# Four attention layers on one core: first layer recomputed in fewer products, third layer's projection folded into its values, reciprocals as logarithm and exponential, maxima turned by transfers, all of the last layer's sums on POOL

## The chip, the cores and the metric

The kernel runs on one core of a Trainium2 chip. The time is the device time of one execution in microseconds. Six engines matter: PE (TensorE, matrix products), DVE (VectorE), ACT (ScalarE), POOL (GpSimd), SP (SyncE, which here only issues transfers) and the DMA engines. Each runs its own list of instructions in order; they meet through semaphores.

## The reference

Eight images of 256 channels and 1024 positions go through four layers. Each layer adds to or replaces `x`, and each holds a softmax over 1024 by 1024 scores. Cut to what is computed:

```python
# layer 0 (L = 32 latent channels, P = 128 concepts)
th, ph, g = conv1x1(x, w_theta), conv1x1(x, w_phi), conv1x1(x, w_g)
lat = softmax(th.T @ ph) @ g.T              # (1024, 32), then reshaped as (32, 1024)
sa = gamma_sa * conv1x1(lat, w_o) + x
enc = conv1x1(sa, w_theta)
lat2 = softmax(enc.T @ concepts.T) @ concepts   # again reshaped
x = gamma_moca * conv1x1(lat2, w_o) + sa
# layer 1
q, k, v = Wq @ x + bq, Wk @ x + bk, Wv @ x + bv         # 32, 32, 256 channels
x = gamma * (v @ softmax(q.T @ k).T) + x
# layer 2
h = group_norm(x); q, k, v = qkv_w @ h + qkv_b          # 256 channels each
x = x + proj_w @ (softmax(q.T @ k / 16) @ v.T).T + proj_b
# layer 3: 8 heads of 32 channels
h = group_norm(x); q, k, v = per head of wq h + bq, wk h + bk, wv h + bv
o = softmax(q.T @ k) @ v for each head
x = layer_norm(wo @ o + bo) * ln_gamma + ln_beta + x
```

The reshape of the latents in layer 0 is not a transpose: a (1024, 32) array is read as (32, 1024), so that the elements change their place among partitions and columns.

## The kernel before

**Tiling.** An image lies in SBUF as 128 partitions by 2 channel halves by 1024 columns. PSUM is one tensor `ps` of 8 banks of 512 fp32 columns. Banks 0 to 3 belong to the layers 0 to 2 ("front"), banks 4 to 7 to layer 3 ("back"). Every attention works on tiles of 128 keys (`NT` = 8) and two halves of 512 queries (`IC` = 2). Scores are made with the keys on the partitions, exponentiated by ACT into SBUF (`pr` in front, `prb` in back) and used as the moving operand of a product with the values. The sum over the keys is gathered by elementwise additions of these tiles (`acc`, `accb`) and one product with ones at the end of each half (`sum_weights`, L690 in front, L869 in back). The numerators are divided by this sum afterwards.

**Exact scores.** Queries and keys are split into a high and a low part (to_stacks, low_stacks, high_parts, low_parts). In layers 0, 1 and 3, three such parts are stacked on 96 partitions, and row 96 (`ROW`) holds minus the maximum of each query, so that one product of 97 rows gives the shifted score (`stacked_scores`, L544). The maxima come first: `max_tile` (L530) makes a tile of scores with the queries on partitions and DVE takes the negated maximum of 1024 columns (`maximum`, L1141), 8 per head. To get them into row 96, PE multiplies each column by the identity (`shift_rows`, L537, 8 products per head) and ACT copies row 96 of the result (`shift_row`, L931).

**Layer 0.** `values0` (L580) makes the values with 16 products of 32 columns. `weigh` (L596) weighs them in four column groups, ACT copies the parts, PE turns and adds them (L604) and sums the weights by a column of ones (L609), DVE divides (`latents`, L1159, L1162), SP writes the latents to DRAM and reads them back in the other shape (L367, L370), PE multiplies by the output weights (`times_wo`, L617) and DVE adds the input (L1173). The second half repeats this with the concepts: projection (L511), scores (L640), softmax, transposition (L646), product (L651), the DRAM trip and `times_wo` again.

**Layers 1 and 2.** `chunks` runs 4 double steps per half: PE makes two banks of scores, ACT exponentiates both in one instruction of 1024 columns (L942), PE weighs (L672), POOL adds (`add_step` L431, `fold` L437). One pair of banks is in use, so the next scores wait for the exponentials. DVE takes the reciprocal of the sums (L1191, 512 columns) and multiplies (L1195). Layer 2 then projects (L511 with `o2`) and DVE adds to `xm` (L1290).

**Layer 3.** Heads are done in two groups of four (`u` = 0, 1). For each: SP copies the parts into the stacks (L390, 24 transfers), 32 maxima, four `shift_rows`, then 16 steps (`steps(u)`): four scores into three turning banks, four exponentials (L1027), weighing of the step before in four column groups (L857). DVE adds the weights of two heads (`add_weights`, L1316) and POOL those of the other two (L485): 7 additions per half on each. ACT's exponentials of step s wait for the additions of step s-2, because `prb` holds two steps. `normalise` takes the reciprocal (L1323) and multiplies (L1327). At the end come the projection, the layer norm with its square root on ACT (L1081) and reciprocal on DVE (L1360), and the output.

**Order.** Layers 0 to 2 of batch b+1 and layer 3 of batch b are written as two generators on each engine. The table `ORDER` says, per engine, how many pieces of the one and of the other follow each other; `merged` reads it. In the last batch the back runs alone, its second group's maxima merged with the first group's steps ("last").

## Time and profile before

| | us |
|---|---|
| median of 3 runs | 3452.57 (3451.96 to 3454.35) |
| the profiled execution, time | 3459.3 |
| the profiled execution, span | 3457.5 |

| engine | busy, share of span |
|---|---|
| PE | 3090.3 us, 89% |
| DVE | 2004.5 us, 58% |
| ACT | 1174.9 us, 34% |
| POOL | 1030.6 us, 30% |

The mean granted TensorE clock is 0.857 of full speed. A window row gives a stretch in us from the start, its length, and then for each engine the busy time and the number of instructions, the granted clock (1.0 is 2.4 GHz, 0.5 is 1.2 GHz), and the DMA share and rate. A group row gives source line, engine, operation, output and inputs, shapes, count, then busy time in us and mean ns of one, then the idle time of the engine before them and what ended it. One fp32 product counts as two PE instructions.

### The profile page before, as it was taken

Reading aid. Unit: us, or ns where it says so; the run is one execution under the profiler, and the core shown is the slowest. Engines: PE = TensorE matmul, PEld = TensorE weight load, DVE = VectorE, ACT = ScalarE, POOL = GpSimd, SP = SyncE. Lnnn points to the kernel's source line nnn. Section 1 sums busy time; section 2 is a strip of 40 time slices with the busy share of each in tenths; the row PEclk is TensorE's granted clock in tenths of the full one; section 3 lists DMA queues with packets and bytes.
Section 4 is the critical chain, followed back from the end, with each engine's and each line's share of the span. In section 5 each row is a group of like instructions: output and inputs, shape, how many; then the busy total and the mean of one; then the engine's idle time right before and its main releaser. Section 6 shows DMA issues by size and latency. Waiting matters only on the chain.

```text
span 3457.5 us, 27670 instructions
## 1 busy us (share of the span) xinstructions
PE 3090.3 (89%) x10884; PEld 1609.0 (47%) x10884; DVE 2004.5 (58%) x1853; ACT 1174.9 (34%) x1736; POOL 1030.6 (30%) x435
## 2 busy tenths in 40 slices
PE   5778998989989898999989899898998989898886
PEld 2344544545445453545435454454545544354432
DVE  2242657555574656647574565746567465655576
ACT  1111251522525233342424325242243423243145
POOL 2002141411605115141233215150161422423044
PEclk7689797986989879898879979798798987899688
DMA  1000101020100201002010110102010020100300
GB/s 53 3 0 25 40 4 37 1 73 7 37 0 1 73 7 37 1 22 55 4 37 1 41 36 7 33 1 73 7 37 1 7 67 6 37 1 25 71 2 13
DMA packets 44803, 84.77 MB, mean 25 GB/s; under 512 B 24160, under 2 KB 24320, under 8 KB 43392
## 3 DMA queue, kind: packets, MB, share of 16 engines
q1 hardware_dynamic: 42496, 74.61, 8.7%
q0 software_dynamic: 2176, 8.39, 0.8%
q8 instruction: 85, 1.39, 0.2%
q14 instruction: 46, 0.38, 0.0%
HBM read 13.76 MB, written 10.49 MB: 7 GB/s over the span
## 4 chain that ended last, share of the span: by engine, by line
PE 68%; DVE 17%; ACT 6%; SPq 4%; issue 2%; POOL 1%; DMA 1%; DVEq 0%; ACTq 0%; POOLq 0%
PE ps L511 14%; PE ps L672 11%; PE ps L544 9%; PE ps L530 7%; DVE nmx_b L1141 6%; PE ps L857 6%; PE ps L765 5%; SPq L390 4%; PE ps L617 3%; PE ps L519 3%; PE ps L537 3%; DVE accb L1316 2%; DVE rden L1191 2%; PE ps L596 2%; PE ps L746 2%
## 5 line engine op out<-in xcount | busy, mean ns | idle before, releaser
L1027 ACT ACTIVATE prb<-ps 128x512 f32<-128x512 f32 x1024 | 556.5, 599 | 542.3 <-PE ps L544 474.5
L1141 DVE TENSOR_REDUCE nmx_b<-ps 128x1 f32<-128x1024 f32 x512 | 605.8, 1216 | 128.7 <-PE ps L530 127.4
L485 POOL TENSOR_TENSOR accb<-accb,prb 128x1024 f32<-128x1024 f32 x192 | 514.1, 2678 | 169.7 <-ACT prb L1027 161.5
L530 PE MATMUL ps<-ks,qs 96*128 96x512 f32 x960 | 457.1, 593 | 84.5 <-DVE nmx_b L1141 70.5
L1316 DVE TENSOR_TENSOR accb<-accb,prb 128x1024 f32<-128x1024 f32 x192 | 360.3, 1877 | 227.3 <-ACT prb L1027 225.0
L672 PE MATMUL ps<-pr,x_in 128*128 128x512 f32 x1024 | 488.5, 612 | 0.0
L485 POOL TENSOR_TENSOR accb<-prb 128x1024 f32<-128x1024 f32 x32 | 98.2, 3068 | 1164.8 <-ACT prb L1027 1111.6
L544 PE MATMUL ps<-qs,ks 97*128 97x512 f32 x960 | 393.9, 480 | 23.9 <-ACT prb L1027 12.1
L530 PEld LDWEIGHTS ps<-ks,qs 96*128 96x128 f32 x960 | 212.2, 259 | 332.3 <-DVE nmx_b L1141 254.9
L544 PEld LDWEIGHTS ps<-qs,ks 97*128 97x128 f32 x960 | 172.5, 195 | 278.6 <-ACT prb L1027 162.2
L942 ACT ACTIVATE pr<-ps 128x1024 f32<-128x1024 f32 x192 | 196.4, 1023 | 302.8 <-PE ps L544 215.5
L672 PEld LDWEIGHTS ps<-pr,x_in 128*128 128x128 f32 x1024 | 201.0, 197 | 194.4 <-issue 173.0
L857 PE MATMUL ps<-prb,vb 128*32 128x512 f32 x2048 | 278.4, 616 | 0.9 <-ACT prb L1027 0.9
L431 POOL TENSOR_TENSOR acc<-acc,pr 128x1024 f32<-128x1024 f32 x80 | 195.6, 2445 | 264.8 <-ACT pr L942 262.6
L511 PE MATMUL ps<-h,w 128*128 128x512 f32 x384 | 206.5, 690 | 40.6 <-DVE h L1195 38.2
L1141 DVE TENSOR_REDUCE nmx_f<-ps 128x1 f32<-128x1024 f32 x192 | 226.6, 1214 | 18.2 <-PE ps L746 13.7
L511 PE MATMUL ps<-hb,w 128*128 128x512 f32 x384 | 196.9, 661 | 24.5 <-ACT hb L951 22.9
L765 PE MATMUL ps<-q2k 128*128 128x512 f32 x768 | 199.7, 396 | 0.0
L431 POOL TENSOR_TENSOR acc<-pr 128x1024 f32<-128x1024 f32 x40 | 94.8, 2370 | 300.3 <-ACT pr L942 300.3
L1191 DVE RECIPROCAL rden<-ps 128x512 f32<-128x512 f32 x32 | 107.4, 3355 | 132.6 <-PE ps L690 131.2
L1323 DVE RECIPROCAL rdenb<-ps 128x512 f32<-128x512 f32 x32 | 107.3, 3354 | 100.5 <-PE ps L869 100.4
L765 PEld LDWEIGHTS ps<-q2k 128*128 128x128 f32 x768 | 146.3, 190 | 37.9 <-issue 6.0
(148 smaller groups left out, 3296.2 us busy)
## 6 DMA issues: line engine op xcount, KB each, us to landing
qs<-part SPq DMA_DIRECT2D x180, 128.0 KB, 2.3
ks<-part SPq DMA_DIRECT2D x180, 128.0 KB, 2.4
x_in<-in_x POOLq DMA_DIRECT2D x8, 1024.0 KB, 5.8
xd<-xm SPq DMA_DIRECT2D x8, 1024.0 KB, 4.6
out<-prb SPq DMA_DIRECT2D x32, 256.0 KB, 2.0
q2k<-part SPq DMA_DIRECT2D x24, 128.0 KB, 2.4
w<-in_weights SPq DMA_DIRECT2D x1, 2592.0 KB, 10.4
latents<-rden SPq DMA_DIRECT2D x16, 128.0 KB, 2.3
```

Of the source, the lines that this page charges most:

```text
L431: pool.tensor_tensor(into[:], pr[:, (s - 1) % 2, :, :] if jg == 1 else into[:], pr[:, s % 2, :, :], ALU.add).then_inc(summed[n].sem, 1)
L485: pool.tensor_tensor(accb[:, 2:4, :], prb[:, (s - 1) % 2, 2:4, :] if j == 1 else accb[:, 2:4, :], prb[:, s % 2, 2:4, :], ALU.add)\
L511: mm = pe.matmul(ps[0:m, bank, :], wcol(name, kt, m0, m), src[:, kt, cols(ic)], start=kt == 0, stop=kt == CH - 1)
L530: mm = pe.matmul(ps[:, bank + jc, :], queries[0:STACK, tile(it)], keys[0:STACK, cols(jc)], start=True, stop=True)
L544: return pe.matmul(ps[:, bank, :], keys[0:ROW + 1, tile(jt)], queries[0:ROW + 1, cols(ic)], start=True, stop=True)
L672: mm = pe.matmul(ps[:, 2 + ch, :], v[:, jt, tile(ch)], pr[:, s % 2, j, :], start=jt == 0, stop=jt == NT - 1)
L765: mm = pe.matmul(ps[:, j, :], kpart[:, kt, keys], qpart[:, kt, cols(ic)], start=False, stop=kt == CH - 1 and kpart is kl2)
L857: mm = pe.matmul(ps[L * g:L * g + L, back0 + 2, :], vb[:, jt, L * (QUAD * u + g):L * (QUAD * u + g + 1)], prb[:, s % 2, g, :], start=jt == ...
L942: act.activation(pr[:, s % 2, :, :], ps[:, 0:2, :], ACT.Exp).then_inc(exped[n].sem, 1)
L1027: act.activation(prb[:, s % 2, g, :], ps[:, turn3[score_use(s, g) % 3], :], ACT.Exp)\
L1141: dve.tensor_reduce(nmx[side][:, head, it:it + 1], ps[:, bank:bank + 2, :], AX.XY, ALU.max, negate=True).then_inc(max_sb[n].sem, 1)
L1316: dve.tensor_tensor(accb[:, 0:2, :], prb[:, (s - 1) % 2, 0:2, :] if j == 1 else accb[:, 0:2, :], prb[:, s % 2, 0:2, :], ALU.add)\
```

## The change

**Layer 0** is rebuilt. The projection gives theta twice, g and phi in one product of 128 rows; DVE copies g to SBUF and PE turns it with 8 transposes into `vgo`, whose other 32 columns are ones, so that the weighing product also makes the sums and the additions on POOL go. The parts are added by two products with two stacked identities. DVE's 32 by 32 transpose, reading PSUM in the order of the reshape, takes the place of the trip through DRAM; the reciprocal is of 32 by 32 elements. `enc` is not made from `sa`: theta of the input is kept in rows 32 to 63 of `lat_r`, and a prepared product of the output weights, theta and the concepts adds the latents' share, so the first product with the output weights, the first residual and the projection of `sa` go. One product with the output weights (`wo_con` of 64 rows, both gammas in it) does both residuals.

**Layers 1 to 3.** The value biases move behind the softmax (into `bo2`, `bo3`, and the residual of layer 1), gamma of layer 1 into its value weights, and the third layer's projection into its value weights at the start of the program; after `chunks` DVE adds straight to `xm`. `chunks` now runs single tiles, with two banks of scores taking turns and four of weights, weighing two tiles behind. ACT copies the numerators to `tmp`. Every reciprocal of sums becomes ln on PSUM and exp(-x) on ACT (`invert`); group and layer norm use ln and exp(-x/2); a table set that holds ln and exp is loaded at the start. Half of the value copies move from DVE to ACT.

**Maxima of layer 3.** DVE transposes the 128 by 32 block of maxima in blocks of 32 by 32 and rounds it; SP copies it by four transfers into row 96 of the four heads. The 64 products and 8 ACT copies per batch go.

**Sums of layer 3.** POOL does both additions of a step; DVE none.

**The next image** is loaded as soon as layer 0 has added its residual, into `x_in`, since the values of layers 1 and 2 now lie in `h`. The `ORDER` table is new for all engines.

The core of the diff:

```diff
-                pool.tensor_tensor(accb[:, 2:4, :], prb[:, (s - 1) % 2, 2:4, :] if j == 1 else
-                                   accb[:, 2:4, :], prb[:, s % 2, 2:4, :], ALU.add)\
-                    .then_inc(summed_pool.sem, 1)
+                for pair in (slice(0, 2), slice(2, 4)):
+                    pool.tensor_tensor(accb[:, pair, :], prb[:, (s - 1) % 2, pair, :] if j == 1 else
+                                       accb[:, pair, :], prb[:, s % 2, pair, :], ALU.add)\
+                        .then_inc(summed_pool.sem, 1)
```

```diff
+            def invert(b, n, count, bank, into):
+                act.wait_ge(total[n].sem, total[n].at(b, count))
...
+                act.activation(into, ps[:, bank, :], ACT.Ln).then_inc(logged[n].sem, 1)
+                yield
+                act.wait_ge(logged[n].sem, logged[n].at(b, count))
+                act.activation(into, into, ACT.Exp, scale=-1.0).then_inc(inverse[n].sem, 1)
```

```diff
+            def shift_rows(b, u, last):
+                queries = stacks3(u, last)[0]
+                sp.wait_ge(max_r[3].sem, max_r[3].at(b, u + 1))
+                for q in range(QUAD):
+                    row = queries[ROW:ROW + 1, :, :].rearrange("p g (i q c) -> p q (g i) c", q=QUAD, c=L)
+                    sp.dma_start(bf32(row[:, q, :, :]), bf32(nmx_r["back"][L * q:L * q + L, :])).then_inc(shift_in.sem, 16)
+                yield
```

```diff
-                pe.wait_ge(normed[2].sem, normed[2].at(b, 4))
-                for k in range(4):
-                    ic, ch = divmod(k, CH)
-                    project(k, "o2", h, P * ch, P, ic).then_inc(l2_proj.sem, 1)
-                yield
```

```diff
             def latents(b, n):
-                sums = ps[:, 2, 0:NT * (L + 1)].rearrange("p (n c) -> p n c", n=NT)
-                dve.reciprocal(rlat[:], sums[:, :, L]).then_inc(l0_rlat.sem, 1)
-                yield
...
+                dve.wait_ge(l0_lat_ps.sem, l0_lat_ps.at(b, n + 1))
+                dve.transpose(turned[n], ps[0:2 * L, 2 * n:2 * n + 2, :].rearrange("p i n -> p (i n)")
+                              .rearrange("p (l r) -> p r l", l=L)).then_inc(l0_turned.sem, 1)
+                yield
+                dve.wait_ge(l0_turned.sem, l0_turned.at(b, n + 1))
+                dve.reciprocal(inv_sums[n], turned[n][sums[n], :].rearrange("p (r c) -> p r c", r=L)[:, :, 0])\
+                    .then_inc(l0_inv.sem, 1)
+                yield
+                dve.wait_ge(l0_inv.sem, l0_inv.at(b, n + 1))
+                dve.tensor_tensor(lat_r[mixed[n], :].rearrange("p (r c) -> p r c", r=L),
+                                  turned[n][mixed[n], :].rearrange("p (r c) -> p r c", r=L),
+                                  inv_sums[n].unsqueeze(2).broadcast_to([L, L, L]), ALU.mult)\
+                    .then_inc(l0_lat.sem, 1)
```

```diff
+                for t in range(STEPS):
+                    ic, jt = divmod(t, NT)
+                    if t == 0:
+                        pe.wait_ge(shift_sb[n].sem, shift_sb[n].at(b, 1))
+                    scores(take_turn(use01(t)), jt, ic).then_inc(scored[n].sem, 1)
+                    yield
+                    if t > 1:
+                        weigh(t - 2)
+                        yield
```

## Rows read from the trace of the kernel before

**Rows 1.** The page: busy time, share of the span and instructions of each engine.

```profile
PE 3090.3 (89%) x10884; PEld 1609.0 (47%) x10884; DVE 2004.5 (58%) x1853; ACT 1174.9 (34%) x1736; POOL 1030.6 (30%) x435
```

**Rows 2.** Windows: one steady stretch, cut into the last layer's five stages.

```profile
1264.00:1356.00 92.00, 86.23 (x326) 39.54 (x326) 50.80 (x36) 45.41 (x77) 51.17 (x19) 0.90 0.12 28
1356.00:1426.00 70.00, 61.05 (x163) 30.95 (x162) 56.67 (x63) 11.46 (x14) 5.98 (x3) 0.76 0.04 10
1426.00:1516.00 90.00, 89.12 (x401) 50.74 (x399) 45.20 (x33) 46.29 (x76) 43.98 (x18) 1.00 0.00 1
1516.00:1561.00 45.00, 39.83 (x111) 18.62 (x110) 25.22 (x18) 14.21 (x19) 10.31 (x6) 0.92 0.14 47
1561.00:1673.50 112.50, 103.19 (x371) 58.13 (x371) 70.42 (x82) 31.16 (x35) 16.78 (x8) 0.81 0.17 43
```

**Rows 3.** Groups by form: DVE, ACT and POOL instructions that set prices.

```profile
L1141 DVE TENSOR_REDUCE nmx_b<-ps 128x1 f32<-128x1024 f32 x512 | 605.8, 1216 | 128.7 <-PE ps L530 127.4
...
L1027 ACT ACTIVATE prb<-ps 128x512 f32<-128x512 f32 x1024 | 556.5, 599 | 542.3 <-PE ps L544 474.5 <-DVE accb L1316 36.0 <-POOL accb L485 27.8
...
L485 POOL TENSOR_TENSOR accb<-accb,prb 128x1024 f32<-128x1024 f32 x192 | 514.1, 2678 | 169.7 <-ACT prb L1027 161.5
...
L1191 DVE RECIPROCAL rden<-ps 128x512 f32<-128x512 f32 x32 | 107.4, 3355 | 132.6 <-PE ps L690 131.2
...
L948 ACT ACT_TABLE_LOAD x16 | 20.5, 1283 | 0.3
```

**Rows 4.** Groups by form: PE instructions that the change removes in whole or part.

```profile
L511 PE MATMUL ps<-h,w 128*128 128x512 f32 x384 | 206.5, 690 | 40.6 <-DVE h L1195 38.2 <-ACT h L951 2.4
...
L617 PE MATMUL ps<-pr,wo_con 32*128 32x512 f32 x128 | 114.2, 1070 | 10.5 <-DMA pr<-latents 10.5
...
L537 PE MATMUL ps<-ident_r,nmx_rb 128*128 128x128 f32 x512 | 79.8, 316 | 4.5 <-DVE part L1136 1.7 <-DVE nmx_rb L1147 1.5 <-ACT qs L931 1.3
...
L511 PE MATMUL ps<-xm,w 128*32 128x512 f32 x64 | 38.8, 763 | 0.8 <-DVE xm L1173 0.8
...
L580 PE MATMUL ps<-w,x_in 128*128 128x32 f32 x256 | 29.8, 276 | 0.0
```

**Rows 5.** Timeline, PE: start and duration in us; last row with the wait before it.

```profile
1265.79 7.19 PE L617 MATMUL ps<-pr,wo_con 32*128 32x512 f32 x8
...
1284.47 1.06 PE L857 MATMUL ps<-prb,vb 128*32 128x512 f32 x8
...
1502.18 1.53 PE L765 MATMUL ps<-q2k 128*128 128x512 f32 x6
...
1512.57 3.60 PE L672 MATMUL ps<-pr,x_in 128*128 128x512 f32 x8
...
1551.82 9.33 PE L511 MATMUL ps<-h,w 128*128 128x512 f32 x16 [4.77 <-DVE h L1195]
```

**Rows 6.** One line: SP's issues of the stacks, ns min/median/max, and their landing.

```profile
L390 SPq DMA_DIRECT2D ks<-part x180: 507/591/1701, 354.2 to 3218.3; - x180
...
DMA to landing us min/median/max: 2.2/2.3/3.7
```

**Rows 7.** One line each: POOL's and DVE's additions, duration ns min/median/max.

```profile
L485 POOL TENSOR_TENSOR accb<-accb,prb x192: 2349/2398/3350, 465.8 to 3423.9; 128x1024 f32<-128x1024 f32 x192
...
L1316 DVE TENSOR_TENSOR accb<-accb,prb x192: 1207/1696/3236, 463.5 to 3421.6; 128x1024 f32<-128x1024 f32 x192
```

**Rows 8.** Windows of the head: first, second and third layer of batch 0.

```profile
23.00:127.00 104.00, 74.71 (x212) 35.98 (x213) 22.17 (x26) 17.67 (x17) 16.62 (x8) 0.63 0.03 5
127.00:207.00 80.00, 58.88 (x145) 29.92 (x144) 28.97 (x28) 13.82 (x13) 16.61 (x8) 0.80 0.00 0
207.00:342.00 135.00, 112.51 (x351) 66.86 (x352) 40.22 (x58) 23.35 (x26) 17.34 (x9) 0.90 0.04 16
```

**Rows 9.** Windows of the last batch: first round with maxima, second round.

```profile
3278.00:3362.00 84.00, 68.43 (x275) 28.57 (x275) 67.19 (x51) 36.75 (x68) 38.16 (x14) 0.84 0.08 18
...
3370.00:3431.00 61.00, 48.80 (x212) 16.01 (x212) 41.21 (x17) 34.60 (x66) 40.33 (x14) 0.87 0.00 1
```

778 lines of the change are left out of this document (403 added, 375 removed), and 22 rows, old and new, of the table ORDER.

## The prediction

> **What bounds the kernel now.** I read the page first, then the stages of one steady stretch, then the groups of instructions by form. The page [rows 1] shows PE busy 89% of the span, DVE 58%, ACT 34%, POOL 30%. So most of the time is PE's own work.
>
> The run has a head (batch 0's first three layers alone, 0 to 342 us), seven stretches in which the first three layers of batch b+1 are merged with the last layer of batch b, and the last layer of batch 7 alone (3188 us to the end). One stretch lasts 409.5 us, and [rows 2] cut one into five stages by the last layer: round one of its steps (92 us), the second group's maxima (70), round two (90), its end (45), and group norm to the first group's maxima, which is also where the first layer runs (112.5). The reader should see two kinds of stage. Round two has PE busy 89.1 of 90 us at full clock: it is PE's work and nothing else. The maxima stages have PE at a granted clock of 0.76 to 0.81 in the mean of its two levels (2.4 GHz is 1.0, 1.2 GHz is 0.5) and DVE busy 57 of 70 and 70 of 112.5. There the order is set by DVE's reductions (32 of 1.216 us are 39 us, [rows 3]), by short serial steps, and by PE at the low clock.
>
> **What goes on PE.** Per batch, each group's busy time of [rows 4] divided by 8:
> - The third layer's projection is folded into the value weights. Its 16 instructions are a third of the 48 per batch in the group of 206.5 us: 8.6 us.
> - The first layer loses its values product (29.8 / 8 = 3.7), one of two products with the output weights (114.2 / 2 / 8 = 7.1), the 32-row projection (38.8 / 8 = 4.9), and the turning of the parts and the sums by a column of ones, 32 instructions as short as the 32 of the values product: 3.7 again.
> - The last layer loses the 64 small products that spread the maxima (79.8 / 8 = 10.0).
> Removed: 8.6 + 3.7 + 7.1 + 4.9 + 3.7 + 10.0 = 38.0 us. Added: eight small transposes and two fp32 products of 512 columns for the parts, with two more in place of the sixteen 33-column ones. An fp32 product of this width is two instructions, and eight of them take 3.60 us at full clock [rows 5], so 0.45 each, 0.9 at the low clock. Four such products replace or add 3.6 to 7.2 us, minus the sixteen short ones (1.9), plus 0.9 for the transposes: 2.6 to 6.2. I take 4.5. Net 33.5 us of PE busy per batch, 268 us over eight. This is the core of the forecast. It is 8% of the span, and only in idle PE time would it be worth nothing.
>
> **What goes around PE.** The 512-column reciprocals on DVE (3.36 us each, ten per batch) become a logarithm and an exponential on ACT, each priced at the 0.599 us of the nearest ACT row: 1.2 us and one hand-over of about 0.2. Where PE waits for them this gives back some 2 us: it waited 4.77 us before the projection of the third layer [rows 5], every batch, and that wait goes with the projection. Next late there is the fourth layer's group norm, because PE goes on with the next first layer, which waits only for the last normalisation. The table loads of 1.283 us (16 in the group of [rows 3], 47 in all) disappear if one set holds all functions used. They are 60 us of ACT over the run, mostly beside other work, and I count 1 us per batch within the stages below. The Trainium skill, ScalarE: Activation LUTs, section "What ACT_TABLE_LOAD costs", puts a switch at about 2.66 us with its drain; by that the same 47 would be 125 us of ACT, and the sum would not change, since ACT is a third busy.
>
> The trip of the latents through DRAM goes: two transfers in a row, twice per batch. In the head PE idles for it; in the stretches the maxima fill it. In its place stand two DVE transposes of 64 x 1024 and two 32-partition products over 1024 columns. The trace has no such transpose. Bounds: the nearest 1024-column DVE rows give 1.22 us as the floor [rows 3], a reciprocal's pace of 6.6 ns per column gives 6.7 us as the ceiling. I take 1.3, since it writes one element per lane and column as the reduction reads one. The shift's eight ACT copies per batch go with it, and instead SP issues four transfers per group. An issue holds SP 0.59 us and lands 2.3 us later [rows 6], so 4 x 0.6 + 2.3 + 0.5 of DVE = 5.2 us from the last maximum to the first step. PE has 6.9 us (first group) and 8.6 us (second) of projections placed ahead of the steps in its order, so this is hidden in the stretches. Without that cover it would cost 5.2 where the shift products now cost 8. Queued behind it on SP are only the next stacks, which need the round's scores anyway.
>
> **What POOL pays.** The last layer's sums now split between DVE and POOL, 14 additions each per round. Afterwards POOL makes all 28. An addition takes POOL 2.349 us at least, 2.398 in the median and 3.35 at most [rows 7]; DVE's own twin runs from 1.207 to 3.236. Both are slow where they overlap, which is the trace's sign that the two engines hold each other up. With DVE's additions gone I take 2.4: 28 x 2.4 = 67 us per round. Into each round also fall three such sums of the front layer and a fold of half the width, 3.5 x 2.4 = 8.4 us. POOL starts after the second step (6 us in) and stands still for some 3 us between the two halves, until PE has summed the first one. Together 6 + 67 + 8.4 + 3 + 1 = 86 us. The Trainium skill, SBUF — State Buffer, section "Who interferes with whom", says that a DVE instruction with two SBUF inputs and a GpSimd instruction reading SBUF exclude each other for the whole instruction. The trace agrees (1.207 against 3.236 us), and by that rule POOL's 2.4 is right only while few such DVE operations are left; the new products with the inverse sums and the residual additions are eight of that kind for each of two layers.
>
> **Stage by stage, one stretch.** PE's instructions of each stage, counted from the order tables of both kernels and priced at full clock by [rows 5] (1.53 us for six one-pass products, 1.4 where more follow at once; 3.60 for four of fp32; 1.06 for a step's four weighings), come to 78 us of PE in round one before and after, 87 to 96 in round two (the new order puts more of the third layer there), 44 to 34 in the second maxima, 35 to 26.5 at the end, and 75 to 60 in the first-layer stage.
> - Round one: PE 78, POOL 86. It is now POOL's stage. 92 becomes 87.
> - Second maxima: DVE needs 39 for maxima and 10 for the front layer, and 8.6 of projections follow. 70 becomes 60.
> - Round two: PE 96, POOL 86, with steps of 3 to 4 us of PE in the first half where POOL needs 4.8, so some stall: 90 becomes 100.
> - End and first-layer stage, 157.5 together: the chain from the last sum to the fourth layer's input falls from 15 us (reciprocal, projection) to 6.5. The end keeps 30. The rest is 35 us to the first maximum and 46 of DVE (39 and the first layer's 7) plus 9 to the steps, about 91. Sum 127.5, minus 30.
> A stretch: 409.5 - 5 - 10 + 10 - 30 = 374.5, so 35 us less. Seven: 245.
>
> **Head.** [rows 8]: first layer 104 us at clock 0.63, where PE is busy only 75. Two double transfers (5.2 us of PE idle each), half of the serial chain after the weighing and the ping-pong of scores and exponentials go: 104 becomes 69. Second layer 80 becomes 65, since scores now run one bank ahead and a 3.36 us reciprocal goes. Third 135 becomes 115: projection 7, waits 8, ping-pong 5. The folded products at the start add 5. Together 65 less.
>
> **Last batch alone.** [rows 9]: the second round takes 61 us now, no front layer beside it. POOL alone is 6 + 67 + 3 = 76, so +18 with its sum. The first round, 84 us with the maxima in it, becomes about 81; the shift stages give 5, the last normalisation and layer norm (three reciprocals in a row) 8. Sum +2.
>
> **Sum.** The profiled execution's span is 3457.5 us and its time 3459.3, 0.2% over the median of 3452.57. 3457.5 - 65 - 245 + 2 = 3149.5, plus 1.8 around it 3151, and by the same 0.2% a median of 3145.
>
> **Rivals.**
> 1. POOL stays slow. DVE's remaining two-input operations and waits keep an addition at its present mean, 2.68 us [rows 3]. Then a round is 28 x 2.68 + 8.4 + 10 = 93 for POOL, round two near 104, so +10 per stretch and +8 at the end: 3225. For it: the 3.35 us maxima of [rows 7]. Against it: the overlap partner is gone. The Trainium skill, GPSIMD Engine Reference, section "4.1 Engine selection", advises VectorE for element-wise sums and calls GpSimd about 2 times slower; by the trace it is 2.35 against 1.21. At a contended 3.3 us throughout, rounds would be 110 each and the gain would go: about 3440.
> 2. The first-layer stage does not shrink. PE has less to do there, and the clock was at the low level where PE idled for DVE. If that stage is held by DVE and hops and keeps 17 of the 30 us, the time is 3145 + 119 = 3265.
> 3. Logarithm and exponential do not share a table. Twelve logarithms per batch would bring 24 loads, 31 us of ACT, half on the path: 3145 + 120 = 3265.
> 4. Slower: POOL's pace drops PE's clock. PE runs in order, so a late POOL holds the front layers too, and in both rounds PE would idle enough to be granted the low level. Their 174 us of full-clock work take 249 us at a mean clock of 0.70 instead of 187: +62 x 7, so 3580. It eats the gain of 35 per stretch from a mean clock of about 0.78 down. Against it: round one now is granted 0.90 and round two 1.00 [rows 2], and PE's share there stays near 90%.
> 5. Better: the orders fit, and the second maxima and the first-layer stage reach DVE's floor, 12 us less per stretch: 3060.
>
> **How the numbers follow.** Forecast 60%, rival 1 14% (of which 2% for the lost gain), rival 2 10%, rival 3 3%, rival 4 4%, rival 5 9%. The unknown sizes (transpose 1.2 to 6.7, POOL 2.35 to 2.68, stages by some 5 us each) give 3085 to 3225 around the forecast. To leave out no more than 2 in 10 I reach to rivals 2 and 3 and stop short of 5: 3080 to 3265. Faster by over 0.2%, about what a measurement of this kernel can tell: 95%, within 1%, slower 4%.
>
> **What would show it.** PE busy falls by 230 to 300 us; a stretch lasts 362 to 385 us; POOL busy rises to about 1210 us (8 x (56 x 2.4 + 17)) with additions near 2.4 us; POOL is among the releasers of the last layer's exponentials in round one; round one stays near 87 and round two grows; there is one table load; the last round alone grows by 15 to 20 us. The prediction is wrong if additions stay above 2.6 us, if the granted clock of the rounds drops below 0.85, or if the first-layer stage stays above 100 us.

## The result and the profile after

The changed kernel takes 3152.7 us (median of four runs, 3147.6 to 3157.4) against 3453.5 of the kernel before beside it: a ratio of 0.913, 95% interval 0.911 to 0.914. The forecast was 3145. Its profiled execution has a span of 3151.9 us; the sum of the prediction made 3149.5 of it.

The page of the changed kernel, busy time by engine, answers to [rows 1]. PE lost 297.5 us, DVE 601, and POOL gained 306:

```profile
PE 2792.8 (89%) x9636; PEld 1421.5 (45%) x9636; DVE 1403.5 (45%) x1525; ACT 1208.5 (38%) x2073; POOL 1336.3 (42%) x595
```

The same steady stretch as in [rows 2], cut at the same events (round one, second maxima, round two, end, first-layer stage), by windows. Columns: window, length, busy us and instructions of PE, PE's weight loads, DVE, ACT, POOL, then granted clock, DMA share, GB/s:

```profile
1119.90:1206.00 86.10, 79.67 (x335) 36.35 (x334) 21.57 (x20) 50.14 (x89) 75.86 (x34) 1.00 0.18 46
1206.00:1267.00 61.00, 52.11 (x122) 25.20 (x120) 52.47 (x62) 9.95 (x17) 7.25 (x4) 0.78 0.03 6
1267.00:1361.00 94.00, 94.00 (x419) 52.91 (x421) 16.27 (x16) 49.43 (x90) 75.15 (x33) 1.00 0.00 1
1361.00:1400.00 39.00, 33.52 (x89) 15.91 (x81) 18.66 (x25) 16.00 (x27) 8.14 (x4) 0.91 0.15 55
1400.00:1494.70 94.70, 81.01 (x244) 44.70 (x245) 65.42 (x69) 24.98 (x37) 0.00 (x0) 0.80 0.15 34
```

Round two has no idle PE time at all: it is PE's. Round one has POOL busy 75.9 of 86.1 and PE idle for 6.4 at full clock: nearly balanced. The two stages with maxima still stand at a clock of 0.78 to 0.80, as before, only shorter.

The head, by windows that end with each layer's last residual addition (99.7, 170.6 and 276.9 us; in the kernel before 124.0, 204.5 and 329.2, so [rows 8] cut it 3 to 13 us later):

```profile
23.90:99.70 75.80, 56.38 (x140) 25.25 (x140) 25.72 (x30) 16.94 (x25) 0.00 (x0) 0.61 0.00 0
99.70:170.60 70.90, 59.70 (x148) 30.39 (x148) 21.80 (x21) 19.12 (x29) 17.88 (x9) 0.84 0.04 15
170.60:276.90 106.30, 92.87 (x290) 56.23 (x291) 27.76 (x42) 23.32 (x37) 16.78 (x8) 0.92 0.00 0
```

The last batch alone, both rounds by windows, answers to [rows 9]. POOL is busy 66 us in each, and in the second PE stands idle for 20.8 us and is granted a clock of 0.69:

```profile
2969.00:3047.50 78.50, 65.02 (x272) 26.69 (x270) 39.81 (x35) 36.73 (x69) 66.20 (x28) 0.84 0.14 31
...
3049.00:3129.50 80.50, 59.74 (x208) 17.60 (x208) 2.13 (x2) 36.58 (x69) 65.91 (x28) 0.69 0.00 1
```

The groups by form that answer to [rows 3] and [rows 4]; columns as there:

```profile
L498 POOL TENSOR_TENSOR accb<-accb,prb 128x1024 f32<-128x1024 f32 x384 | 904.4, 2377 | 74.6 <-ACT prb L1079 58.7
...
L1079 ACT ACTIVATE prb<-ps 128x512 f32<-128x512 f32 x1024 | 562.0, 599 | 478.9 <-PE ps L581 313.5 <-POOL accb L498 161.1 <-PE ps L862 1.3
...
L1266 DVE TENSOR_TENSOR tmp<-tmp,rden 128x512 f32<-128x512 f32 x64 | 83.6, 1328 | 674.3 <-ACT rden L960 674.3
...
L1232 DVE STREAM_TRANSPOSE pr<-ps 64x1024 f32<-64x1024 f32 x16 | 19.8, 1237 | 32.4 <-PE ps L653 21.7 <-PE ps L671 10.7
...
L957 ACT ACTIVATE rden<-ps 128x512 f32<-128x512 f32 x32 | 19.2, 598 | 56.1 <-PE ps L702 56.1
...
L914 ACT ACT_TABLE_LOAD x1 | 1.3, 1283 | 0.7 <-PEq L1461 0.7
...
L548 PE MATMUL ps<-h,w 128*128 128x512 f32 x256 | 129.0, 653 | 2.5 <-ACT h L1000 2.5
...
L548 PE MATMUL ps<-x_in,w 128*128 128x512 f32 x64 | 47.5, 910 | 33.1 <-DVE tmp L1266 32.9 <-DVE vec L1189 0.2
```

POOL's additions take 2.377 us where they took 2.678 beside DVE's. The exponentials of the last layer now wait 161 us for POOL where they waited 64 for POOL and DVE together. That looks like a heavy price; the experiments show how little of it is one.

The time is given back in three places. From start to the first step of the last layer: 442.3 to 372.7 us, 69.6 less. Seven periods between first steps: 405.4 to 370.9 in the mean, 241.5 less (the period of batch 6 included, in which no further first layer runs). The last batch from its first step on: 177.6 to 182.8, so 5.2 more.

### The profile page after: what moved, and what is told of

Its sections match the earlier page's. It is cut to its first block, busy times and chain, and to the rows that moved or that the text cites. A ratio compares the mean times of both kernels' runs of the same rounds, so it can differ in the third digit from the quotient of the medians.

```text
span 3151.9 us, 25364 instructions
## 1 busy us (share of the span) xinstructions
PE 2792.8 (89%) x9636; PEld 1421.5 (45%) x9636; DVE 1403.5 (45%) x1525; ACT 1208.5 (38%) x2073; POOL 1336.3 (42%) x595
## 4 chain that ended last, share of the span: by engine, by line
PE 64%; DVE 17%; POOL 9%; ACT 5%; issue 2%; SPq 1%; DMA 1%; DVEq 0%; POOLq 0%; ACTq 0%
PE ps L548 12%; PE ps L695 10%; PE ps L581 9%; POOL accb L498 9%; DVE nmx_b L1215 8%; PE ps L567 7%; PE ps L862 6%; PE ps L780 5%; PE ps L556 5%; PE ps L637 2%; PE ps L766 2%; SPq L404 1%; DVE nmx_f L1215 1%; DVE tmp L1266 1%; ACT prb L1079 1%
## 5 line engine op out<-in xcount | busy, mean ns | idle before, releaser
L498 POOL TENSOR_TENSOR accb<-accb,prb 128x1024 f32<-128x1024 f32 x384 | 904.4, 2377 | 74.6 <-ACT prb L1079 58.7
L498 POOL TENSOR_TENSOR accb<-prb 128x1024 f32<-128x1024 f32 x64 | 153.6, 2420 | 1291.0 <-ACT prb L1079 1288.8
L695 PE MATMUL ps<-pr,h 128*128 128x512 f32 x1024 | 486.8, 600 | 8.2 <-ACT tmp L976 8.2
L1266 DVE TENSOR_TENSOR tmp<-tmp,rden 128x512 f32<-128x512 f32 x64 | 83.6, 1328 | 674.3 <-ACT rden L960 674.3
L948 ACT ACTIVATE pr<-ps 128x512 f32<-128x512 f32 x384 | 219.8, 597 | 239.5 <-PE ps L581 140.6
L695 PEld LDWEIGHTS ps<-pr,h 128*128 128x128 f32 x1024 | 191.2, 191 | 209.7 <-issue 182.3
L447 POOL TENSOR_TENSOR acc<-acc,pr 128x1024 f32<-128x1024 f32 x64 | 152.4, 2380 | 210.1 <-ACT pr L948 210.1
L581 PE MATMUL ps<-q2k,ks 97*128 97x512 f32 x256 | 138.6, 576 | 11.7 <-ACT q2k L936 6.3
L1371 DVE TENSOR_TENSOR hb<-hb,rdenb 128x512 f32<-128x512 f32 x32 | 31.6, 986 | 228.2 <-ACT rdenb L960 228.2
L548 PE MATMUL ps<-h,w 128*128 128x512 f32 x256 | 129.0, 653 | 2.5 <-ACT h L1000 2.5
```

The source lines that it names most:

```text
L447: pool.tensor_tensor(acc[:], before if jg == 1 else acc[:], now, ALU.add).then_inc(summed[n].sem, 1)
L498: pool.tensor_tensor(accb[:, pair, :], prb[:, (s - 1) % 2, pair, :] if j == 1 else accb[:, pair, :], prb[:, s % 2, pair, :], ALU.add)\
L548: mm = pe.matmul(ps[0:m, bank, :], wcol(name, kt, m0, m), src[:, kt, cols(ic)], start=kt == 0, stop=kt == CH - 1)
L581: return pe.matmul(ps[:, bank, :], keys[0:ROW + 1, tile(jt)], queries[0:ROW + 1, cols(ic)], start=True, stop=True)
L695: mm = pe.matmul(ps[:, 2 + ch, :], v[:, jt, tile(ch)], pr[:, t % 4, :], start=jt == 0, stop=jt == NT - 1)
L948: act.activation(pr[:, t % 4, :], ps[:, bank, :], ACT.Exp).then_inc(exped[n].sem, 1)
```

## The experiments

Stage lengths below are counted in every kernel from the last layer's first exponential of a round to the end of its last sum product, medians over seven stretches: round one 92.0 before and 85.5 after, second maxima 73.8 and 62.1, round two 87.2 and 93.9, the rest (end and first-layer stage) 153.6 and 130.6. Ratios are to the kernel before, run beside each.

### Does POOL's pace cost anything?

**Sums split again, everywhere.**

```diff
-                            for pair in (slice(0, 2), slice(2, 4)):
-                                pool.tensor_tensor(accb[:, pair, :], ...)
+                            pool.tensor_tensor(accb[:, 2:4, :], ...)
...
+                        if s % NT:
+                            add_weights(u, s)      # DVE: accb[:, 0:2, :]
+                            yield
```

> The changed kernel with one part undone: the last layer's sums are split again between DVE (heads 0 and 1) and POOL (heads 2 and 3) in all batches, with DVE's order table worked out anew for it. Theory (PE's work and the serial chain carried the gain; POOL's pace binds only in round one, where PE idles 6.4 of 87 us, and in the last batch alone): round one 87 becomes 84 to 87, round two stays at 94 within 2, because there PE is the bound, and the last batch gives 15 to 18 back. Together 3120 to 3150 us against 3152.7. Rival (POOL's pace is paid in every round): 4 to 8 us less in each of 14 rounds and 16 in the last batch, 3025 to 3080 us. Second rival (the additions on DVE meet POOL's again at 3 us and more, and DVE's front-layer work is late behind them): slower, 3170 to 3250 us. POOL busy falls from 1336 to some 900 us, DVE busy rises by 300 to 500.

It took 3134.8 us, ratio 0.907 (0.906 to 0.908), 18 to 20 us less than the change. Round one is 84.1 (1.4 less), round two 94.3 (0.4 more), and the second round of the last batch 56.3 for 80.1. DVE's additions ran from 1.207 to 3.387 us, and POOL's rose from 2.377 to 2.631 us. PE stays at 2788 us busy, and 16.9 of the gain are in the last batch. The first theory holds; in the stretches the exponentials' waiting for POOL was not time lost.

**Split in the last batch only.** DVE's order table for the last batch is new with it.

```diff
+                            for pair in (slice(2, 4),) if last else (slice(0, 2), slice(2, 4)):
...
+                        if last and s % NT:
+                            add_weights(u, s)
```

> The changed kernel, with the sums split between DVE and POOL only in the last batch, where no front layer runs beside them. Theory (there POOL alone sets the pace: 28 additions of 2.4 us a round against 14): both rounds of the last batch become 12 to 18 us shorter where they are POOL's, less what round one has in maxima; 3152.7 becomes 3125 to 3142 us. Rival (the last batch's rounds are longer for another reason, such as the exponentials on ACT or the single bank turn): within 3 us of 3152.7.

It took 3131.5 us (3130.2 to 3133.9), ratio 0.906 (0.905 to 0.908): 21 us faster than the change. The interval overlaps that of split_all, 0.906 to 0.908: splitting the last batch's sums alone gains all that splitting them everywhere does, and no kernel here that makes the sums in full is faster. Windows of its last batch, both rounds:

```profile
2965.00:3045.00 80.00, 63.55 (x271) 26.45 (x269) 65.53 (x49) 36.53 (x68) 37.17 (x14) 0.88 0.13 30
3049.50:3106.50 57.00, 46.62 (x208) 15.01 (x208) 40.40 (x15) 36.02 (x69) 41.25 (x14) 0.86 0.00 1
```

All of the gain is in the second round: PE idles 10.4 us there instead of 20.8, and the same 208 instructions take 46.6 us instead of 59.7, at a clock of 0.86 and not 0.69. The first round doesn't gain (80 against 78.5): DVE now has additions and the second group's maxima there, 65.5 us of work. My expectation of 12 to 18 in both rounds was wrong in its split, right in its sum.

**POOL made light.** Its second pair of additions on 8 columns only, so part of the sums is left out.

```diff
+                                n_c = IW if j == 1 or pair.start == 0 else 8
```

> The changed kernel, with the second pair of POOL's additions (heads 2 and 3, from the second on) done for 8 of 512 columns only: part of the sums is left out, all waits stay. POOL's work in a round falls from 67 to some 38 us. Theory: what POOL's pace costs in all comes back: 4 to 6 us in round one and 1 to 3 in round two of each of seven stretches, and 15 us in each of the last batch's rounds, together 60 to 90 us: 3060 to 3095. Rival (POOL's pace costs nothing in the stretches): only the last batch, 3120 to 3135. Second rival (POOL's lateness holds the clock of the rounds down too): below 3040 us, and the granted clock of round two rises from 0.80.

It took 3121.0 us, ratio 0.903 (0.901 to 0.905), 32 to 34 less than the change: the first rival's number, not mine. Windows of a stretch's rounds one and two, and of the last batch's:

```profile
1111.80:1195.00 83.20, 79.26 (x335) 36.30 (x334) 19.01 (x20) 50.28 (x89) 50.03 (x34) 1.00 0.16 41
1257.00:1351.00 94.00, 94.00 (x420) 52.56 (x419) 17.57 (x16) 49.09 (x91) 51.28 (x33) 1.00 0.00 1
2957.50:3027.50 70.00, 62.09 (x271) 26.39 (x269) 38.39 (x35) 36.91 (x69) 39.97 (x28) 0.88 0.15 34
3030.50:3093.50 63.00, 53.10 (x209) 16.81 (x209) 1.67 (x1) 35.90 (x69) 40.28 (x28) 0.77 0.00 1
```

With 25 us of POOL's work gone, round one is 2.4 us shorter and round two not at all, and the rest of the stretch lost 1.9 of that again (132.5 for 130.6). So in the stretches POOL's pace costs next to nothing, and in the last batch alone 26 us by the two rounds. Another 5 us of this trace's gain lie ahead of the last layer's first step (367.7 for 372.7 us), where the edit changes nothing: differences of that size between two traces say little. The second rival can't be read as it stands: the 0.80 that it names is not the clock of round two, which is 1.00 in the changed kernel and in this one.

### The same additions in the old kernel

**POOL makes all sums in the kernel before.**

```diff
-                        dve.tensor_tensor(accb[:, 0:2, :], ...)
+                    pass
...
+                            for pair in (slice(0, 2), slice(2, 4)):
+                                pool.tensor_tensor(accb[:, pair, :], ...)
```

> The kernel before with one part of the change alone: POOL makes all the last layer's additions, in its old order, and DVE none. Theory (POOL's pace binds only where PE has less work than POOL): in the old rounds PE has 82 and 89 us of work against POOL's 86, so 0 to 4 us per round in the stretches, and 15 to 18 in each of the last batch's rounds: 3452.6 becomes 3470 to 3530 us. Rival (the additions on DVE held up the maxima and the front layer): 3400 to 3445 us. Second rival (POOL late in every round): above 3540.

It took 3665.7 us, ratio 1.061 (1.059 to 1.063): 210 us slower, the third of the three cases. Round one went from 92.0 to 106.6, round two from 87.2 to 94.1, the rest from 153.6 to 159.2; a period is 24 us longer, and the last batch 33. Windows of rounds one and two; then PE's and POOL's timelines at the start of round one (start, duration, and the wait before in brackets):

```profile
1304.60:1411.20 106.60, 93.57 (x333) 40.66 (x332) 28.64 (x22) 45.67 (x76) 76.10 (x33) 0.85 0.13 29
...
1484.50:1578.60 94.10, 87.58 (x391) 47.02 (x389) 24.19 (x16) 42.92 (x73) 75.77 (x33) 0.98 0.00 1
```

```profile
1305.36 7.19 PE L617 MATMUL ps<-pr,wo_con 32*128 32x512 f32 x8
1312.48 1.65 PE L544 MATMUL ps<-qs,ks 97*128 97x512 f32 x3
1313.93 4.67 PE L511 MATMUL ps<-xm,w 128*128 128x512 f32 x8
```

```profile
1323.69 4.69 POOL L485 TENSOR_TENSOR accb<-prb 128x1024 f32<-128x1024 f32 x2 [66.33 <-ACT prb L1025]
```

In round one POOL starts 19.1 us after the first exponential, because PE's order has 7.2 and 4.7 us of front products between the first two steps. From there to its last addition it has 73.8 us of work and some 8 of waits, and the last sum product ends 5.7 us later: together 106.6 us. In the changed kernel it starts after 4.8 us:

```profile
1124.68 4.68 POOL L498 TENSOR_TENSOR accb<-prb 128x1024 f32<-128x1024 f32 x2 [109.67 <-ACT prb L1079]
```

4.8 + 74.4 of work + 5.2 of waits + 1.1 to the end are its 85.5. The kernel before starts its additions as late (after 19.0 us), but with 51 us of work in the round its last one ends after 83 of the 92 us. With 76 it ends after 101 and sets the end of the round, and PE then idles 13 us and works at a clock of 0.85 for 0.90 before [rows 2], 93.6 us busy for 86.2.

**Other order tables for it.** I moved the last layer's steps ahead of the front layer's pieces by up to 18 us in round one, on all engines, once with POOL making all sums and once with the old split.

```diff
 ORDER = {
     ("both", "PE"): (
...
     ("both", "POOL"): (
-        0, 9, 4, 1, 4, 1, 2, 2, 2, 2, 2, 5, 5, 1, 2, 1, 1, 2, 1, 1, 5, 4,),
+        0, 9, 6, 1, 3, 1, 1, 1, 1, 1, 2, 2, 1, 5, 5, 1, 2, 1, 1, 2, 1, 1, 5, 4,),
```

> The kernel before with POOL making all the last layer's additions (as in before_pool_all), and in addition other order tables for the merged part: in round one the last layer's steps are moved up to 18 us ahead of the front layer's pieces, so that the first addition no longer comes 19 us after the first exponential (there PE ran 7.2 and 4.6 us of front products between the first two steps). Theory (with POOL at 76 us of work in a 107 us round the loss of 24 us per stretch comes from where the order lets POOL start and stand, not from its pace as such): round one 106.6 becomes 90 to 96 us, round two stays near 94; 3665.7 becomes 3570 to 3610 us. Rival (POOL's pace by itself is what costs): round one stays above 103 us and the time above 3640.

> The kernel before, its additions split between DVE and POOL as they were, with the same new order tables for the merged part as reordered_pool_all: the order alone. Theory (PE has 82 us of work in round one and 86.4 busy of 92, so an order can give it at most 5 us): within 30 us of 3452.6, and the difference to reordered_pool_all is 110 us or less where the old order had 213. Rival (the new order is better or worse by itself, whoever adds): the two reordered kernels differ by the same 213 us.

They took 3713.1 us (ratio 1.074) and 3615.5 us (1.047). In the traces the first addition now comes 13.3 us after the first exponential instead of 19.1. Round one by windows, POOL alone and split:

```profile
1322.60:1436.40 113.80, 97.00 (x333) 41.81 (x332) 26.38 (x22) 45.47 (x76) 75.92 (x33) 0.80 0.13 28
```

```profile
1301.00:1416.00 115.00, 99.29 (x333) 43.15 (x332) 53.61 (x36) 45.49 (x76) 48.96 (x19) 0.79 0.12 28
```

My tables are bad ones: they cost 160 us with nothing else changed, where I had expected less than 30. The expectation that round one would fall to 90 to 96 failed too: POOL starts 5.8 us earlier in it and it is 7 us longer, so the start alone doesn't make the length. The two reordered kernels differ by 98 us, within the 110 that I had given; of these 31 are in the last batch, and the others are in round two and in the rest of the stretches. Two things follow. Under this order POOL's 27 us of added work cost round one nothing (113.8 against 115.2 us), under the old order 14.6, under the changed kernel's 1.4: what POOL's additions cost is a matter of the order around them. And with the old split 333 PE instructions, as many as before, take 99.3 us for 86.2, at a clock of 0.79 for 0.90, after 15.7 us of idle time instead of 5.8: PE's idle time is paid twice. A table with which the old kernel carries POOL's sums for nothing I didn't find. So I gave the changed kernel the late start instead.

**A late start for POOL in the changed kernel.**

```diff
+                            if s == 1 and u == 0:
+                                for k in range(6):
...
+                                    pool.tensor_tensor(accb[:, 0:2, :], prb[:, 0, 0:2, :], prb[:, 1, 0:2, :],
+                                                       ALU.add).then_inc(late_done.sem, 1)
```

> The changed kernel; in round one of each batch POOL makes six more additions of 1024 columns (6 x 2.38 = 14.3 us, their result is overwritten) after the exponentials of the second step and before its first addition of sums, so that these start 19 us after the round's first exponential, as in before_pool_all, where they start after 4.8 us in the changed kernel. Theory (a round lasts POOL's start + its work + its waits as soon as that sum is above PE's own): round one goes from 85.5 (4.8 + 75.9 + 5) to 97 to 101 us, the last batch's from 78 to 92, and PE's clock in it falls below 0.95; 3152.7 becomes 3240 to 3270 us. Rival (POOL catches up, since PE, ACT and POOL have other gaps in the round; the 14.6 us of before_pool_all came from the old order's other places): round one below 92 us, the time below 3200. Round two stays at 94 in both.

It took 3302.9 us, ratio 0.956 (0.954 to 0.957): 150 more. POOL's timeline at the start of round one, and the round by windows:

```profile
1160.53 14.44 POOL L504 TENSOR_TENSOR accb<-prb 128x1024 f32<-128x1024 f32 x6 [111.18 <-ACT prb L1089]
1175.05 4.65 POOL L508 TENSOR_TENSOR accb<-prb 128x1024 f32<-128x1024 f32 x2
```

```profile
1155.70:1261.00 105.30, 85.71 (x335) 38.27 (x334) 19.98 (x20) 50.49 (x89) 89.56 (x40) 0.87 0.14 34
```

Round one is 106.0 us, 20.5 more for 14.4 of delay; round two is 93.9 as before. The rival is out: POOL does not catch up. The theory's 97 to 101, and with it the 3240 to 3270 for the whole, was too low: POOL's own waits in the round grew from 5 to 11 or 12 us, and PE, at 0.87 of its clock for 1.00, is busy 6 us more with the same 335 instructions. So a late start alone makes of 85.5 us the 106 that before_pool_all has. The last batch's round one went from 78.3 to 93.2 us, near the 92 expected. That the late start is the whole of it in the old order too is not shown by this, since the two orders differ elsewhere.

### What the other parts give

Each of these undoes one part in the changed kernel and keeps its order tables. They give a part's worth beside the rest of the change, and do not add up to the 301 us. The first layer's new form has no run of its own; its share is only what PE's fewer instructions in [rows 4] and the shorter first layer of the head say, and so it is argued and not shown.

**Maxima spread by PE and ACT again.**

```diff
-                sp.dma_start(bf32(row[:, q, :, :]), bf32(nmx_r["back"][L * q:L * q + L, :]))...
+                        for it in range(NT):
+                            mm = pe.matmul(ps[...], nmx_r["back"][...].broadcast_to([P, P]), ident_r[:], ...)
+                        act.activation(stacks3(u, last)[0][ROW:ROW + 1, g, :], ps[...], ACT.Copy)
```

> The changed kernel with the maxima of the last layer spread by 32 small PE products and four ACT copies per group again, in place of DVE's transpose and SP's four transfers. Theory (PE's work on the path counts at full length): 10 us of PE per batch return, and of the 5.2 us transfer chain nothing was visible: 8 to 10 us per batch, 3152.7 becomes 3215 to 3235 us. Rival (PE waits for the maxima and for the stacks at that place anyway, so the products are hidden): 3150 to 3175 us.

It took 3269.0 us, ratio 0.946 (0.945 to 0.948): 116 more, 14.5 per batch, above my 8 to 10. The products and the copies, by form:

```profile
L834 PE MATMUL ps<-ident_r,nmx_rb 128*128 128x128 f32 x512 | 71.5, 297 | 5.5 <-ACT qs L1107 3.0 <-issue 2.5
L1107 ACT ACTIVATE qs<-ps 1x1024 fp32r<-1x1024 f32 x60 | 58.0, 1010 | 24.6 <-PE ps L834 24.6
```

The products are 8.9 us per batch. The whole of PE is busy 112 us more (2905.0), not 71.5: 40 come from the rest. In four of the seven stretches round one took 93 us instead of 85.5, in three 86.8, though no product was added there. One of each kind by windows:

```profile
762.70:855.70 93.00, 89.03 (x335) 39.25 (x333) 17.57 (x17) 50.51 (x89) 75.53 (x34) 0.87 0.15 39
1149.70:1236.60 86.90, 81.33 (x335) 37.07 (x334) 18.89 (x17) 50.19 (x89) 75.55 (x34) 0.97 0.18 44
```

The same number of instructions takes 89.0 us at a clock of 0.87 and 81.3 at 0.97, where the changed kernel has 79.7 at 1.00. So part of the loss is a lower clock in a stage that holds none of the added products. Why the clock is lower in some stretches than in others stays open. The remaining loss is in the second maxima (65.3 for 62.1 us), in the rest of the stretch (137.0 for 130.6), in the last batch (10.5) and ahead of the first step (5.6). The undone part runs in tables made for the change, so 116 us is its worth here and not in general.

**The transfers in eight halves.**

```diff
+                    for k in (0, 64):
+                        sp.dma_start(bf32(row[:, q, 16 * k // 64:16 * k // 64 + 16, :]), ...)
```

> The changed kernel with the four transfers that bring a group's maxima to the shift row cut into eight halves: 4 x 0.6 = 2.4 us more of SP per group, the same bytes. Theory (the transfers of both groups are hidden behind 6.9 and 8.6 us of projections in PE's order): within 6 us of 3152.7 over the whole, the last batch included. Rival (the chain from the last maximum to the first step is on the path): 2.4 us in each of 16 groups, 3152.7 becomes 3185 to 3200 us.

It took 3163.2 us, ratio 0.916 (0.914 to 0.917), some 10 us more, 0.7 per group of the 2.4 added to SP. That is hardly clear of the noise: the interval touches the change's own, 0.911 to 0.914. The transfers are mostly hidden, at most a little less than I said.

**No shared table set.**

```diff
-            act.preload_act_table_set("natural_log_exp_and_others")
```

> The changed kernel without the one instruction that loads a set of ACT's tables holding logarithm, exponential and copy together; everything else stays. Theory (the shared set is part of the gain): a load of 1.28 us returns around each logarithm, 16 to 20 per batch, 20 to 25 us of ACT per batch, part of it on the path: 3152.7 becomes 3200 to 3300 us. Rival (the set is chosen so that it holds anyway, or ACT has room for every load): within 10 us, with few loads in the trace.

It took 3289.0 us, ratio 0.952 (0.950 to 0.954): 136 more. There are 193 loads, 24 per batch, 248 us of ACT, and the kernel lost more than half of that; two groups of them by form:

```profile
L956 ACT ACT_TABLE_LOAD x64 | 82.1, 1283 | 24.9 <-DVE hb L1370 23.9
L959 ACT ACT_TABLE_LOAD x57 | 73.1, 1283 | 1.0
```

The second maxima go from 62.1 to 68.3 us and the rest from 130.6 to 140.2; round one takes 1.2 us more and round two no more. An ACT that is 38% busy doesn't hide the loads that stand in a serial chain. Rival 3 had 120 us for this.

**Reciprocals back on DVE in the second and third layer.** The first layer keeps its own reciprocals of 32 by 32 elements.

```diff
-                act.activation(into, ps[:, bank, :], ACT.Ln)...
-                act.activation(into, into, ACT.Exp, scale=-1.0)...
+                        dve.reciprocal(rden[:], ps[:, total_use01(ic) % 2, :])...
```

> The changed kernel, with the inverse of the sums of the first three layers taken by a 512-column reciprocal on DVE again (six per batch at 3.36 us), the two ACT functions in their place gone; the last layer keeps logarithm and exponential. Theory (the hand-over on the path is what the logarithm buys): PE waits for DVE behind the last chunk of each of three layers, 2 to 3.4 us each, and the front layer's other DVE work is 20 us longer per batch, partly beside the maxima, where DVE is the bound: 6 to 14 us per batch, 3152.7 becomes 3200 to 3265 us. Rival (the reciprocals lie beside PE's other work): within 10 us. The PE idle of 5.0 us behind the last product with the inverse sums should grow by 2 to 3 us per batch.

It took 3186.8 us, ratio 0.922 (0.920 to 0.924): 34 more, 4.3 per batch, under my 6. The trace has four such reciprocals per batch (32 in all, 107.3 us), not the six of my expectation, so DVE's added work is 13 us per batch and not 20. Most of the loss is in the second maxima (65.7 for 62.1 us), where DVE is the bound and this stands among the maxima (timeline of DVE):

```profile
1236.83 5.75 DVE L1219 TENSOR_REDUCE nmx_b<-ps 128x1 f32<-128x1024 f32 x5 [0.75 <-PE ps L567]
1242.49 3.35 DVE L1271 RECIPROCAL rden<-ps 128x512 f32<-128x512 f32 x1
```

Of the rest, 6.5 us are in the head (first step at 379.2 for 372.7 us); the rounds and the end are the same within 0.2. PE's wait behind the last product with the inverse sums, which was to grow by 2 to 3 us, went from 5.02 to 5.41. So behind a chunk, the pair on ACT brings PE little, and what counts is that DVE keeps its maxima going.

**The third layer's projection, its work alone.** The result is left unused.

```diff
+                if again:
+                    pe.wait_ge(normed[2].sem, normed[2].at(b, 4))
+                    for k in range(4):
+                        project(2 + k % 2, "o2", h, P * (k % 2), P, k // 2)...
```

> The changed kernel with the work of the third layer's projection added behind its last weighing: 8 fp32 products of 512 columns (16 PE instructions) that wait for the last normalisation, and the residual additions wait for them (the result of the products is left unused). Theory (PE's work counts at full length, and so does the wait ahead of it): 8.6 us at the clock of that stage plus a wait of 2 to 5 us, 10 to 13 us per batch, 3152.7 becomes 3235 to 3260 us. Rival (PE was idle there anyway, for the fourth layer's group norm or for the first layer's products): 3155 to 3190 us.

It took 3216.0 us, ratio 0.931 (0.928 to 0.933): 63 more, 7.9 per batch, where work and wait were to give 10 to 13. Its groups by form show why:

```profile
L549 PE MATMUL ps<-h,w 128*128 128x512 f32 x384 | 205.1, 689 | 40.3 <-DVE tmp L1271 37.9 <-ACT h L1005 2.5
L549 PE MATMUL ps<-x_in,w 128*128 128x512 f32 x64 | 31.0, 629 | 0.2 <-DVE vec L1194 0.2
```

The wait of 4 to 5 us per batch stands before the projection where there is one, and before the next image's first products (`x_in`) where there is none, as the rows of the changed kernel say: 33.1 us there against 0.2, and 35.6 against 40.5 in both groups together. And those products take 0.910 us each in the mean where the wait stands before them in seven of eight batches, 0.629 where it doesn't. By windows, the eight of one batch, in the changed kernel and then here:

```profile
1393.60:1399.60 6.00, 5.94 (x10) 2.62 (x10) 4.00 (x9) 0.01 (x1) 0.00 (x0) 0.63 0.46 175
```

```profile
1417.90:1421.50 3.60, 3.60 (x9) 1.33 (x7) 3.23 (x6) 0.00 (x0) 0.00 (x0) 1.00 0.41 157
```

So of the 76 us of `h` products removed (205.1 to 129.0), 16.5 came back as a lower clock, and nearly the whole wait stayed.

## Why the prediction was right, and where its steps were not

**The core.** PE's work falls, and in rounds and elsewhere that is time: 297.5 us less of PE busy against 268 in the sum. Undoing two of the parts shows it: products put back cost about their own length or more (proj_back 7.9 us per batch for the 8.6 of the projection, shift_pe 14.5 for 8.9), while the additions that POOL took over cost the stretches next to nothing (split_all, light_pool). For the first layer's new form, by the prediction half of the work removed, it is argued. The 30 us above the sum no run separates; the mean granted clock, which rose from 0.857 to 0.882, may be part of them.

**Round one, second maxima, round two.** 87, 60 and 100 foretold; the windows say 86, 61 and 94. Round one is POOL's and PE's alike (28 x 2.38 and the front layer's sums, with a start of 4.8 us: the step held), and with 26 us less of POOL's work it is 2.4 us shorter, so "POOL's stage" was too strong. In round two I added 4 us of stall to 96 us of PE; there is none.

**End and first-layer stage.** 127.5 foretold, 133.7 measured, 39.0 and 94.7. The step that failed is the one that let the wait of 4.77 us [rows 5] go with the projection. The timeline of PE in the changed kernel has it before the next first layer:

```profile
1393.66 5.89 PE L548 MATMUL ps<-x_in,w 128*128 128x512 f32 x8 [5.02 <-DVE tmp L1266]
```

I had said that PE goes on with the next first layer, "which waits only for the last normalisation"; that normalisation is exactly what the wait was for. The wait of 5.0 us stayed, and the products behind it took 2.3 us more than in proj_back, where no wait stands before them. Errors of -6 in round two and +6 here cancel.

**Head.** Foretold 30 (35 less the folding's 5), 15 and 20 us less for the three layers. By the last residual additions they lost 24.3, 9.6 and 18.4, 52.3 together. The first step comes 69.6 us earlier, since the first merged first-layer stage is in it. The serial steps of the first and second layer gave less than I took for them.

**How the sum came out so near.** The prediction cut the run at 342 and 3188 us. The nearest event in both kernels is the last residual addition of the first and of the last image: 329.2 and 3190.4 us before, 276.9 and 2886.4 after. Between these the three terms measure:

| us | foretold | measured |
|---|---|---|
| head | -65 | -52.3 |
| seven stretches | -245 | -251.7 |
| last layer of batch 7 | +2 | -1.6 |
| together | -308 | -305.6 |

The two large terms are right within a fifth. That the span is off by only 2.4 us is luck: the head gave 12.7 us less than foretold and the other two 10.3 more.

**Last batch.** Foretold +2, measured -1.6: 6.8 less up to the first step, 5.2 more from there. The second round went from 58.6 to 80.1 us, +21.5 where I had +18. The stage ahead of the first step, round one and the maxima behind it lost 6.8 + 10.7 us where I had 3 + 5; what follows the last sum went from 28.4 to 22.7, -5.7 for my -8. The signs were right; POOL's term, the one that split_last takes away, was 3 us too small, and the maxima stages gave more.

**POOL.** The addition was sized right (2.377 for 2.4). The total was not: 1336 us instead of 1210. The formula had 17 us of the front layers' sums per batch, but these are 12 additions of 1024 columns and 4 folds, 34 us, of which the other half lies outside the rounds. It moved nothing, since POOL is idle there.

**Prices.** The transpose took 1.237 us for my 1.3, logarithm and exponential 0.60 and 0.63 for 1.2 together, the one table load is there. The kernel before has 48 of them, not 47.

**The rivals.** Slow additions (rival 1) didn't come. Of the 30 us of the end and first-layer stage 24 came (rival 2). The table set holds, and no_preload prices rival 3: 136 us where it had 120. Rival 5 didn't come either: the second maxima took 61 us and the first-layer stage 94.7. Rival 4, POOL's pace and PE's clock, is real: it is what before_pool_all and late_start show, 24 and 20 us per stretch where I had 62. It stayed away here where POOL may start 4.8 us into round one. I had read the new order tables as so much PE work per stage, and not as the place where POOL may start; how much of the early start is theirs, and how much the smaller first layer's, no run separates. I gave it 4% on the right rows (PE's share stays high in the rounds), but these rows didn't exclude it.

## What to carry to other kernels

- Work given to an idle engine can be nearly free if it may start early enough in the stage. Add its start, its work and its waits, and compare the sum with the stage: 4.8 + 74 + 5 cost 2.4 us at most, a start 14 us later cost 20. What others wait for it (161 us here) is no measure.
- PE's work that goes or comes can count more than its length: 71.5 us of small products brought back cost 116, part of it as a lower clock in another stage.
- When a product behind a wait is removed, the wait moves to the next product that needs the same result. Look for that one before counting the wait as gone.
- Where a merged schedule ends in a part without its partner, size that part alone: one choice for all batches cost 21 us in the last one, and a switch there alone won all of that back.

## What the runs showed of the hardware

A DVE product with both inputs in SBUF is slow where it meets POOL's additions, and the same product that reads one input from PSUM isn't. By form, the kernel before with POOL making all sums, then the changed one's own line with minimum, median and maximum in ns:

```profile
L1193 DVE TENSOR_TENSOR h<-ps,rden 128x512 f32<-128x512 f32 x64 | 41.1, 683 | 0.9
```

```profile
L1266 DVE TENSOR_TENSOR tmp<-tmp,rden x64: 677/684/4020, 155.8 to 2884.4; 128x512 f32<-128x512 f32 x64
```

The first stays at 0.673 to 0.692 us with POOL busy for 1462 us of the run, also in the 28 of 64 that overlap one of its additions. The second has the same median, but a mean of 1.328: the 16 of 64 that overlap an addition took 1.7 to 4.0 us each, the other 48 at most 0.693. With the lighter POOL of light_pool the 16 took 1.72 to 1.75 us and the mean was 0.947. The Trainium skill, SBUF — State Buffer, section "Who interferes with whom", says that a DVE instruction with two SBUF inputs contends with a GpSimd instruction that reads SBUF, and one with at most one, outside its 2-port modes, doesn't; these rows agree. So copying the numerators to SBUF on ACT made DVE's next step dearer, by some 41 us over the run; how much of that is on the path no run shows.

The granted clock fell behind idle time in small things too: eight products took 5.89 us at a granted clock of 0.63 behind a 5.0 us wait of PE (after), and 3.60 us at 1.00 without it (proj_back).
